# Two heads on one batch as the unit of an attention, with 512-column products for V

## What is computed

```python
kv = jnp.concatenate([context, latents], axis=1)            # 768 keys per batch
q = rms_norm((latents @ Wq).reshape(b, q_len, 32, 128)...)  # 32 heads of 128
k = rms_norm((kv @ Wk).reshape(b, 768, 8, 128)...)          # 8 key heads, 4 query heads each
v = (kv @ Wv).reshape(b, 768, 8, 128)
scores = jnp.einsum('bhgqd,bhkd->bhgqk', qg, k) * scale
probs = jax.nn.softmax(scores, axis=-1)
out = jnp.einsum('bhgqk,bhkd->bhgqd', probs, v)
x = x + jnp.tanh(g_xattn[0]) * (out @ Wo)
```

## Time and profile before

| | us |
|---|---|
| three runs | 983.24, 985.45, 991.03 |
| median | 985.45 |
| the profiled execution | 984.21 |
| its span, first to last instruction | 982.4 |
| mean granted TensorE clock | 0.996 of full |
| busy PE / DVE / ACT / POOL | 949.6 / 637.1 / 478.6 / 352.9 |

### The profile page before, as it was taken

One profiled execution on the slowest core, in us unless ns is written; L12 is line 12 of the kernel. 1 busy time (PEld: TensorE's weight loads), 2 busy tenths in 40 slices (PEclk: granted clock), 3 DMA queues, 4 the chain that ended last, 5 costly groups with the idle time before them and its releaser, 6 DMA issues. The chain is left out here.

```text
span 982.4 us, 18543 instructions
## 1 busy us (share of the span) xinstructions
PE 949.6 (97%) x6876; PEld 824.3 (84%) x6876; DVE 637.1 (65%) x1107; ACT 478.6 (49%) x937; POOL 352.9 (36%) x256
## 2 busy tenths in 40 slices
PE   6999999999999999999999999999999998999996
PEld 4889989998998899899989989998987876677755
DVE  6777557556754774675567457656744665888856
ACT  4466346535633653464356336534624612656634
POOL 2354325333631633344244316244114721080033
PEclk9989999999999999999999999999999999999999
DMA  6021103202120310032021102200015214933001
GB/s 235 2 76 30 48 1 86 64 0 62 35 53 0 86 60 4 0 94 55 0 75 22 53 0 86 86 0 11 23 42 196 88 40 133 224 64 60 2 1 43
DMA packets 40693, 55.01 MB, mean 56 GB/s; under 512 B 8656, under 2 KB 20560, under 8 KB 40656
## 3 DMA queue, kind: packets, MB, share of 16 engines
q1 hardware_dynamic: 40080, 54.49, 20.0%
q10 hardware_dynamic: 576, 0.00, 0.0%
HBM read 50.22 MB, written 4.26 MB: 55 GB/s over the span
## 5 line engine op out<-in xcount | busy, mean ns | idle before, releaser
L480 DVE TENSOR_TENSOR ptL<-tbank,ptH 128x512 fp32r<-128x512 f32 x192 | 132.2, 689 | 70.2 <-ACT ptH L322 67.8
L322 ACT ACTIVATE ptH<-tbank 128x512 fp32r<-128x512 f32 x192 | 115.5, 602 | 114.4 <-PE tbank L618 114.0
L618 PE MATMUL tbank<-ident,probs 128*128 128x128 f32 x860 | 132.2, 277 | 3.0 <-DVE ptL L480 2.7
L493 DVE TENSOR_REDUCE negmax<-score 128x1 f32<-128x768 f32 x128 | 120.4, 950 | 11.2 <-PE score L80 10.7
L343 ACT ACTIVATE probs<-score,negmax 128x768 f32<-128x768 f32 x128 | 115.5, 903 | 14.9 <-DVE negmax L493 14.9
L78 PE MATMUL obank<-ptH,vH 128*128 128x256 f32 x384 | 121.3, 316 | 0.0
L230 POOL TENSOR_TENSOR rnorm<-sumsq,neg_half 128x2 f32<-128x2 f32 (+1 forms) x80 | 71.4, 896 | 120.5 <-DVE sumsq L453 120.5
L451 DVE TENSOR_REDUCE sumsq<-probs 128x2 f32<-128x256 f32 (+1 forms) x80 | 42.0, 525 | 106.6 <-ACT probs L317 65.7
L618 PEld LDWEIGHTS tbank<-ident,probs 128*128 128x128 f32 x860 | 97.7, 141 | 13.2 <-DVE ptL L480 9.4
L80 PE MATMUL obank<-ptH,vL 128*128 128x256 f32 x384 | 108.8, 283 | 0.0
L79 PE MATMUL obank<-ptL,vH 128*128 128x256 f32 x384 | 108.2, 282 | 0.0
(11 more groups left out here) (282 smaller groups left out, 2240.9 us busy)
## 6 DMA issues: line engine op xcount, KB each, us to landing
wqo_stage<-in_wq SPq DMA_DIRECT2D x9, 1024.0 KB, 5.6
wqo_stage<-in_wo SPq DMA_DIRECT2D x8, 1024.0 KB, 6.9
factors<-r_scratch SPq DMA_DIRECT2D x32, 256.0 KB, 3.9
wkv_stage<-in_wkv SPq DMA_DIRECT2D x9, 512.0 KB, 6.4
a_qS<-q_scratch SPq DMA_DIRECT2D x24, 128.0 KB, 5.0
ctx_stage<-in_ctxT SPq DMA_DIRECT2D x2, 1024.0 KB, 7.1
kS<-k_scratch SPq DMA_DIRECT2D x32, 64.0 KB, 4.0
q_scratch<-qpart SPq DMA_DIRECT2D x16, 128.0 KB, 1.9
```

The costliest lines, as they stand in the source:

```text
L322: act.activation(out, tbank[c % 2][:], ACT.Copy, scale=scale).then_inc(t_hi, 1)
L480: i = dve.tensor_tensor(out, tbank[c % 2][:], f32(hi), ALU.subtract)
L493: dve.tensor_reduce(negmax[:, m:m + 1], score[m % 2][:, 0:SKV], AX.X, ALU.max, negate=True).then_inc(s_max, 1)
L618: i = pe.transpose(tbank[c % 2][:, n * P:(n + 1) * P], block_in, S.ident[:])
```

## The change

A unit `w` is now two heads on one batch (4 units of 4 score tiles). A chunk is one key tile of 128 for the 512 query columns of the unit, so a chunk's product with V is three products of 512 columns, and `obank[w % 2]` is filled by one unit. There are 24 chunks in a turn, as before. `probs` has 8 slots, `ptH` and `ptL` three, `qTH` and `qTL` two heads; `k_rows` and `sq` lie in the later half of `probs`. In the list of every engine a chunk's transposes are followed by the product with V of the chunk two before, and then by one score tile of the next unit (the first four chunks of units 0 to 2). Heads 0 and 1 are transposed at the end of the turn before, heads 2 and 3 inside unit 1. All four score tiles of unit 0 stand between the output projections of the turn before. In the first turn the two late chunks of keys and values are projected in halves, with the second head's transposes and the score tiles between the halves. In the last turn heads 2 and 3 are multiplied together, two row tiles at a time. `pair_rows(oT, w)` is the slice of `oTH` or `oTL` with heads 2(w // 2) and the next one, and the 256 rows of batch w % 2.

```diff
-    qTH, qTL = sb("qTH", [P, GRP, ROWS], f32r), sb("qTL", [P, GRP, ROWS], f32r)
+    qTH, qTL = sb("qTH", [P, 2, ROWS], f32r), sb("qTL", [P, 2, ROWS], f32r)
     kTH, kTL = sb("kTH", [P, NKT * P], f32r), sb("kTL", [P, NKT * P], f32r)
-    NP, NPT = 4, 4
+    NP, NPT = 8, 3
...
+    later = 4 * SKV
+    k_rows = probs_mem[:, later:later + NKT * D0].rearrange("p (t d) -> p t d", d=D0)
+    sq = probs_mem[:, later + NKT * D0:later + NKT * D0 + 3 * 512].rearrange("p (s h d) -> p s h d", s=3, d=D0)
...
-    U, CH = 2 * GRP, 3
-
-    order = [("q", 0), ("k", 0), ("k", 1), ("k", 2)]
-    for u in range(U):
-        if u % 2 == 0 and u // 2 + 1 < GRP:
-            order.append(("q", u // 2 + 1))
-        order += [("p", CH * u + j) for j in range(CH)]
+    PAIRS, CH = GRP, KVT
+
+    order = [("q", 0), ("k", 0), ("q", 1), ("k", 1), ("k", 2)]
+    for w in range(PAIRS):
+        for j in range(CH):
+            order.append(("p", CH * w + j))
+            if w == 1 and j < 2:
+                order.append(("q", 2 + j))
...
+                pool.tensor_tensor(pair_rows(oTL, h), o_norm[:].rearrange("p (h r) -> p h r", h=2), f32(pair_rows(oTH, h)),
+                                   ALU.subtract).then_inc(o_lo, 1)
...
-                pool.wait_ge(pe_s, 16 * g + 3)
+                pool.wait_ge(pe_s, 16 * g + 5)
...
+                    act.wait_ge(pe_t, TC * g + at["p", CH * (m // 4 - 1) - 1] + 1)
...
+                for w in range(PAIRS):
+                    hi_p(g, CH * w)
+                    if w == 1:
+                        hi_q(g, 2)
+                    for t in range(4):
+                        hi_p(g, CH * w + t + 1)
+                        if w == 1 and t == 0:
+                            hi_q(g, 3)
+                        if w + 1 < PAIRS:
+                            exp(g, 4 * w + 4 + t)
+                        if t == 1 and w:
+                            hi_o(g, w - 1)
+                    hi_p(g, CH * w + CH - 1)
 
             def prepare(g):
-                hi_q(g, 0)
-                for i in range(3):
+                for i in range(2):
+                    hi_q(g, i)
                     hi_k(g, i)
+                exp(g, 0)
+                hi_k(g, 2)
+                for m in range(1, 4):
+                    exp(g, m)
...
-            hi_q(0, 0)
+            for i in range(2):
+                hi_q(0, i)
+                hi_k(0, i)
             evac_kv(0, EARLY, True)
-            hi_k(0, 1)
+            for m in range(3):
+                exp(0, m)
             evac_kv(0, EARLY + 1, True)
-            exp(0, 0)
+            exp(0, 3)
             hi_k(0, 2)
-            exp(0, 1)
             turns(act, turn, last)
...
+                dve.wait_ge(pe_pv, 24 * g + CH * (h + 1))
...
+                for w in range(PAIRS):
+                    reciprocals(g, w)
+                    lo_p(g, CH * w)
+                    if w == 1:
+                        lo_q(g, 2)
+                    for t in range(4):
+                        if w == 1 and t == 0:
+                            lo_p(g, CH * w + 1)
+                        if w + 1 < PAIRS:
+                            maximum(g, 4 * w + 4 + t)
+                        if w == 1 and t == 0:
+                            lo_q(g, 3)
+                        else:
+                            lo_p(g, CH * w + t + 1)
+                        if w and t == 0:
+                            normalise_o(g, w - 1)
+                    lo_p(g, CH * w + CH - 1)
...
+                lo_q(g + 1, 1)
                 lo_k(g + 1, 1)
                 add_out(g, 1, obank[1][:])
+                maximum(g + 1, 0)
                 lo_k(g + 1, 2)
-                maximum(g + 1, 0)
-                maximum(g + 1, 1)
+                for m in range(1, 4):
+                    maximum(g + 1, m)
                 add_out(g, 2, obank[0][:])
...
+            lo_q(0, 1)
+            lo_k(0, 1)
             sum_squares(0, RT + EARLY)
             v_lo_part(0, EARLY, True)
-            normalise(0, RT + EARLY, True)
-            lo_k(0, 1)
             maximum(0, 0)
+            maximum(0, 1)
+            normalise(0, RT + EARLY)
+            maximum(0, 2)
             sum_squares(0, NIT - 1)
+            maximum(0, 3)
+            normalise(0, NIT - 1)
             v_lo_part(0, NKV - 1, True)
-            normalise(0, NIT - 1, True)
-            maximum(0, 1)
             lo_k(0, 2)
...
+            def scores(g, w, t):
+                hp, b, m = w // 2, w % 2, 4 * w + t
+                h = 2 * hp + t // 2
+                if b == 0:
                     pe.wait_ge(t_lo, TC * g + at["q", h] + 1)
-                if h == 0:
+                if hp == 0:
                     pe.wait_ge(t_lo, TC * g + at["k", 1 + b] + 1)
-                for m in (2 * u + t for t in tiles):
-                    if u:
-                        pe.wait_ge(s_exp, 16 * g + m - 1)
-                    q = slice(b * SQ + (m % 2) * P, b * SQ + (m % 2 + 1) * P)
-                    for k0, n in ((0, 512), (512, 256)):
-                        keys = slice(b * SKV + k0, b * SKV + k0 + n)
-                        i = mm3(pe, score[m % 2][:, k0:k0 + n], (qTH[:, h, q], qTL[:, h, q]),
-                                (kTH[:, keys], kTL[:, keys]), True, True)
-                    i.then_inc(pe_s, 1)
-
-            def transpose_probs(g, u, j):
+                if m >= 2:
+                    pe.wait_ge(s_exp, 16 * g + m - 1)
+                q = slice(b * SQ + (m % 2) * P, b * SQ + (m % 2 + 1) * P)
+                for k0, n in ((0, 512), (512, 256)):
+                    keys = slice(b * SKV + k0, b * SKV + k0 + n)
+                    i = mm3(pe, score[m % 2][:, k0:k0 + n], (qTH[:, h % 2, q], qTL[:, h % 2, q]),
+                            (kTH[:, keys], kTL[:, keys]), True, True)
+                i.then_inc(pe_s, 1)
+
+            def transpose_probs(g, w, j):
                 if j == 0:
-                    pe.wait_ge(s_exp, 16 * g + 2 * u + 2)
-                transposes(g, ("p", CH * u + j),
-                           [probs[:, (2 * u + qt) % NP, (2 * j + kt) * P:(2 * j + kt + 1) * P]
-                            for kt in range(2) for qt in range(2)])
-
-            def times_v(g, u, j):
-                h, b, c = u // 2, u % 2, CH * u + j
-                if u % 2 == 0 and j == 0 and h >= 2:
-                    pe.wait_ge(o_normed, GRP * g + h - 1)
+                    pe.wait_ge(s_exp, 16 * g + 4 * w + 4)
+                transposes(g, ("p", CH * w + j),
+                           [probs[:, (4 * w + n) % NP, j * P:(j + 1) * P] for n in range(4)])
+
+            def times_v(g, c):
+                w, j = c // CH, c % CH
+                if j == 0 and w >= 2:
+                    pe.wait_ge(o_normed, GRP * g + w - 1)
                 pe.wait_ge(t_lo, TC * g + at["p", c] + 1)
-                for kt in range(2):
-                    key = b * KVT + 2 * j + kt
-                    part = slice(kt * 256, (kt + 1) * 256)
-                    i = mm3(pe, obank[h % 2][:, b * SQ:(b + 1) * SQ], (vH[:, key, :], vL[:, key, :]),
-                            (ptH[:, c % NPT, part], ptL[:, c % NPT, part]), j == 0 and kt == 0, j == CH - 1 and kt == 1)
-                i.then_inc(pe_pv, 1)
+                key = (w % 2) * KVT + j
+                mm3(pe, obank[w % 2][:], (vH[:, key, :], vL[:, key, :]), (ptH[:, c % NPT, :], ptL[:, c % NPT, :]),
+                    j == 0, j == CH - 1).then_inc(pe_pv, 1)
 
             def attend(g):
 
-                for u in range(U):
-                    if u % 2 == 0 and u // 2 + 1 < GRP:
-                        transpose_q(g, u // 2 + 1)
-                    if u == 0:
-                        scores(g, 1, (0,))
-                        transpose_probs(g, 0, 0)
-                        scores(g, 1, (1,))
-                    elif u + 1 < U:
-                        scores(g, u + 1)
+                for w in range(PAIRS):
                     for j in range(CH):
-                        if u == U - 1:
-                            times_v(g, u - 1, j)
-                        if u or j:
-                            transpose_probs(g, u, j)
-                        if 0 < u < U - 1:
-                            times_v(g, u - 1, j)
+                        transpose_probs(g, w, j)
+                        if CH * w + j >= 2:
+                            times_v(g, CH * w + j - 2)
+                        if w == 1:
+                            if j == 0:
+                                transpose_q(g, 2)
+                            if 1 <= j < 4:
+                                scores(g, w + 1, j - 1)
+                            if j == 1:
+                                transpose_q(g, 3)
+                            if j == 3:
+                                scores(g, w + 1, 3)
+                        elif j < 4 and w + 1 < PAIRS:
+                            scores(g, w + 1, j)
...
-                for j in range(CH):
-                    times_v(g, U - 1, j)
```

(82 more changed lines are left out.)

41 lines of the change are left out of this document (10 added, 31 removed).

## The result

The changed kernel took 987.53 us (median of 10 runs, 986.06 to 990.40) beside 983.34 for the kernel before on the same chip: a ratio of 1.0042, with an interval of 1.0022 to 1.0062. It is slower, by 0.4%. (A ratio is taken over all runs of both kernels, and can differ by 0.001 to 0.002 from the quotient of the medians.) The time lies inside the range of the prediction, but the forecast was a gain of 2.7 us, and its sign was wrong. The change is too small to reach the 1% by which the chances were drawn.

What follows compares the result with a forecast made beforehand. PE's instruction list was taken as the bound (busy 949.6 of 982.4 us); -3.8 - 1.3 + 0.8 + 1.6 = -2.7 gave 981.5 from the profiled 984.21, 982.7 by the median, forecast 982.0; range 975 to 989 (chance 0.82).

Steps and rivals of the forecast that it cites:

- Products with V: Attention: 384 products of 256 columns become 192 of 512 per kind, a chunk 0.70 instead of 0.72: -3.8 us.
- Rival D: Products with V: the further 256 columns only stream at 2.4 GHz, 0.227 a product: -7 us, 978.3; chance 0.11.
- Switches: PE between transposes and other work: 27 groups a turn instead of 29, 0.08 each over 8 turns: -1.3 us.
- Stalls: PE's waits in the new units: 1.7 us a turn against 1.6, +0.8 us over 8 turns.
- The end of a turn: Tiles, `q` 1 and exps between the output projections: 0.1 us at one exp, already counted in the stalls' edges.
- POOL: Unit 2's head: normalisation waits for the first output's low part on POOL; no wait, 1.1 us to spare.
- First turn: Opening with late half chunks: work done 1.3 us earlier, but a 2.45 hole and clock fall (+2.9): +1.6 us.
- Last turn: Heads 2 and 3 of two row tiles together: 5.6 us of products cover the wait in both orders, 0.
- Rival A: Unit edges: the chain tile, maximum, exp, transposes waits 0.3 at each of 24 edges: 7.2 us, 988.7; chance 0.13.
- Rival B: Products at 0.2275 (-3.4 more) and no clock fall in the first turn (-2.9): 975.2; chance 0.10.
- Rival C: Products with V: 512 columns cost twice 256, so no gain there: 985.3; chance 0.16.

Runs made afterwards that it cites:

- The pairs: Changed kernel, that kernel with the two `q` groups split over units 0 and 1, and all three edits together, each rerun with 256-column products: 988.11, 978.02, 973.25 us.
- the run without the mix: Changed kernel with the first turn's two late chunks of keys and values projected whole, ahead of all score tiles: 986.54 us, ratio 1.0016.
- all three again: Repeat of the changed kernel with `q` heads 2, 3 split over units 0, 1, last key chunk whole, unit 3's normalisation later: 971.74 us, ratio 0.9886.

## Why the prediction was wrong

The forecast was -2.7, the traces of the changed kernel give +2.7 on average, the medians +2.9 and +4.2. Step by step, from the traces:

*Products with V*, forecast -3.8, measured -1.7 where hardly a hole is left: under half its size. The price of 256 columns was read as 0.12 from rows rounded to 0.01; over whole turns a chunk is 0.009 shorter, not 0.020. A clean chunk is 0.78 with 512 columns (365.50 to 366.28 below) beside 0.79 to 0.80 with 256. In the run with 256 columns five such products take 0.59 (331.52 to 332.11), 0.118 each; 0.002 times 1152 products is 2.3 us, about what is missing, and rows with two decimals could not carry it. The formula I passed over was nearer: by the one in the Trainium skill, "TensorE: Matmul & The Clock Gate", section "Back-to-back issue gap", which that section gives for isolated products and not for a stream of weight loads and products, a chunk is 7.5 ns shorter, 1.4 us in all. The 9 ns measured lie close to it. Rival D needs a chunk to be 0.04 shorter, 0.9 us a turn, and is refuted by the 0.21 (rows 0.23 apart, as at 364.53 and 364.76 below, can't tell 0.227 from the 0.233 that I took; and 0.227 would make -7.5, not the -7 that I wrote). D is what the Trainium skill's price of a weight load ("TensorE: Matmul & The Clock Gate", "LDWEIGHTS") came to here. In the changed kernel itself the gain was only 1.2 (the experiment with 256 columns): I take it that where the next transposes wait for copies, a shorter chunk ahead of them only lengthens the wait. The pairs bear on it in part: over turns 2 to 7 the gain is 0.14 a turn in the changed kernel and still 0.13 without unit 1's holes, and 0.21 once unit 3's is gone too.

*Switches*, forecast -1.3, measured about 0. There are two fewer of them, 0.16 a turn. But a group of transposes right behind another group takes 0.43 where 0.36 was charged (306.83 to 307.26), and four such pairs stand in a turn instead of two: 0.14. The trace of before has that price too (303.85 to 304.28, at the end of turn 3), and I had not used it.

*Stalls*, forecast 1.7 a turn against 1.6. The attention of turn 4 takes 41.5 (324.82 to 366.28), near the 41 forecast. These are the PE rows of turn 4 with the holes:

```profile
310.57 0.66 PE L636 MATMUL tbank<-ident,q_rows 128*128 128x128 f32 x4
311.17 0.66 PE L636 MATMUL tbank<-ident,probs 128*128 128x128 f32 x4
...
335.69 0.61 PE L636 MATMUL tbank<-ident,q_rows 128*128 128x128 f32 x4
336.57 0.66 PE L636 MATMUL tbank<-ident,probs 128*128 128x128 f32 x4 [0.27 <-DVE ptL L489]
336.98 0.48 PE L78 MATMUL obank<-ptH,vH 128*128 128x512 f32 x1
...
337.94 0.51 PE L78 MATMUL score<-kTH,qTH 128*128 128x512 f32 x1
338.28 0.39 PE L79 MATMUL score<-kTL,qTH 128*128 128x512 f32 x1
...
344.15 0.50 PE L78 MATMUL score<-kTH,qTH 128*128 128x512 f32 x1
...
347.85 0.65 PE L636 MATMUL tbank<-ident,probs 128*128 128x128 f32 x4
...
363.81 0.66 PE L636 MATMUL tbank<-ident,probs 128*128 128x128 f32 x4
364.22 0.47 PE L78 MATMUL obank<-ptH,vH 128*128 128x512 f32 x1
364.53 0.39 PE L79 MATMUL obank<-ptL,vH 128*128 128x512 f32 x1
364.76 0.40 PE L80 MATMUL obank<-ptH,vL 128*128 128x512 f32 x1
...
365.50 0.48 PE L78 MATMUL obank<-ptH,vH 128*128 128x512 f32 x1
...
366.28 0.39 PE L78 MATMUL score<-wqH,kvT_hi 128*128 128x512 f32 x1
```

The places are those of the prediction: behind `q` head 2 in unit 1 (335.69 to 336.57 is 0.88 instead of 0.43, forecast 0.5), at the two tiles behind it, at unit 2's first transposes and in unit 3. What was missing is small and came several times. After a hole the following transposes take 0.41 to the first product instead of 0.36, 0.05 each time; the first product of a tile that came late takes 0.34 instead of 0.23 (337.94 to 338.28), 0.11 each time, at two tiles; and the transposes of `k` head 1 at the turn's end, put at 0, come 0.60 behind those of `q` head 1 (310.57, 311.17) instead of 0.43. Added over the rows of turn 4 the stalls are about 2.0, so +0.4 a turn where +0.1 was forecast: some +2.8 in the first seven turns, not +0.8. The experiments on the place of `q` show that the stalls round these groups, most of which were forecast, were the largest piece of the 2.0 and that they were to be had: 1.3 a turn. The small pieces by which 2.0 exceeds the forecast are read from rows, and no run took them away by themselves.

*The end of a turn*, forecast 0: apart from the 0.17 at `k` head 1, which is counted above, right. *POOL*, forecast no wait: right.

```profile
349.08 1.30 POOL L239 TENSOR_TENSOR oTL<-o_norm,oTH 128x512 fp32r<-128x512 f32 x1
```

The low part runs on POOL as before, and DVE is not held behind it: it ends at 350.38, and DVE's next normalisation starts at 351.99, 1.6 behind it where 1.1 was forecast.

*First turn*, forecast +1.6. Against a later turn it has 2.4 more (91.40 - 88.98), before 0.5 (89.36 - 88.87): +1.9. The hole came as forecast (2.45; 2.33 were measured, up to 53.73 instead of 53), then 0.64 for `kTL` 2 (0.95), and the low clock: a tile from 56.33 to 58.41 takes 2.08. This term is off by 0.3. Its reason held only in part: I laid it to the mix, and the run without the mix has the same turn.

*Last turn*, forecast 0 for its own edit: -0.05 as a whole, although it has the products and the unit 1 of the others; what it gains against them was not looked into.

Sum: -1.7 + 0 + 2.8 + 1.9 = +3.0, beside +2.8 and +2.6 in the two traces. So the steps that failed are three, each small and each in the favourable direction: the term for V (-3.8, measured -1.7), the switches (-1.3, measured about 0), and the stalls (+0.8, measured about +2.8). The mechanisms were those forecast; their sizes turned the sign. *Rival A* would have cost 0.3 at each unit's edge through the exps; the waits for `probs` behind ACT sum to 0.2 in the whole kernel. In turn 4 the first transposes of units 1 and 3 start 0.05 late, and those of unit 2 0.26, where 0.3 was forecast. A is refuted. The slower outcome was reached another way. *Rival B* had the clock staying up in the first turn; it did so in the run with the last chunk whole, and turn 1 then cost 3.6 less, but not in the change itself. *Rival C* is refuted by the pairs with 256 columns.

## What to carry to other kernels

Where one engine is 96% busy, a difference of a few nanoseconds in one instruction is read from a whole period of the loop, not from two rounded rows. An operation that is moved brings its buffer's turn-round with it: two groups that share a pair of banks want a chunk of other work between them, and here the place of the two `q` groups (1.3 us a turn) was worth over five times the wider products (0.21). In the first turn of a pipeline, count what stands beside the chain before the first result is used; a long hole there is paid again by the clock behind it.

## What the runs showed of the hardware beside this

- A group of four transposes that follows another directly takes 0.43 us, and 0.36 behind products (306.83 to 307.26; the earlier trace rows).
- Behind a hole the next switch comes about 0.05 later: 0.41 from transposes to the product instead of 0.36 (336.57 to 336.98). No run looked for the reason.
- Three products of 512 columns, each with a new weight, save 0.009 us of some 0.78 a chunk against six of 256 (turns of 87.27 and 87.50).
- In the changed kernel PE worked 1.68 us between 50 and 54, and the clock was at the 1.2 GHz level behind it; with the last chunk whole it worked 1.54 us, with two holes instead of one, and the clock stayed at the 2.4 GHz level. That the second hole made the difference is not shown: in "all three again" the mean clock was 0.72 from 54 to 60, and 1.00 in the first run of the same kernel, so the same order meets the fall in one execution and not in another. The fall cost 1.6 us there.
